# Where the flags of far sampling points are made in a fused deformable-convolution, attention and expert block

## The chip, the cores and the metric

The kernel runs on one core of one Trainium2 chip. The metric is the device time of one execution in microseconds (us). TensorE is called PE below (PEld is its weight load), VectorE is DVE, ScalarE is ACT, GpSimd is POOL and SyncE is SP.

## The reference, cut to what matters

Input x has shape (4, 32, 32, 128): 4 images of 32 x 32 positions with 128 channels. The first layer is a deformable convolution (3 x 3, so 9 points, for each of 8 groups of 16 channels):

```
x1 = silu(bn(depthwise_conv(gn(x))))
offset = x1 @ off_w + off_b                       # (N, H, W, 8, 9, 2)
mask = softmax((x1 @ mask_w + mask_b).reshape(N, H, W, G, P), -1)
samples = _bilinear_sample(img, sg)               # img = gn(x) @ in_w + in_b, padded
out = (samples * m).sum(-1)
return out @ out_w + out_b
```

It is followed by an attention layer over the 1024 positions of each image and by a layer of experts. The change touches the first layer alone.

## The kernel before, in words

The deformable convolution is worked off in 8 chunks of 4 image rows (ROWS = 4, CHUNKS = 8). An offset up to 2 in size (REACH) is handled without a gather: each point's bilinear weight is written as "hats" over 5 taps in x and in y, the mask multiplies the y hats, their outer products are added into a 7 x 7 stencil for each position and group, and the output is the sum over the 49 stencil positions of stencil times shifted input. Points with an offset above 2 in size ("far" points) are few. They are flagged, listed and then repaired by POOL with indirect DMAs.

For a chunk the engines work so:

- DVE ends the silu (finish_silu), so that PE can make 3 x 72 raw offsets and mask logits for each of 4 rows in PSUM (offsets, pair 0).
- ACT (prepare) copies them to SBUF (off), squares the offsets (far_xy, in the tile outer), makes the first 2 of 5 taps of the hats, waits for DVE's shifted logits, takes their exp, makes 3 more taps and finishes all hats with a Relu.
- DVE (mask_logits, masks, weigh_hats) takes the logits' maximum over 9 points, subtracts it in 4 instructions, takes the larger of the two squares, compares it with 4 and so has flags (far); it then sums the exps, divides, and multiplies the y hats.
- DVE (stencils) makes 9 outer products and 8 additions. Between all these instructions stand the products of the chunk before (products), in 28 units of two stencil positions (every fourth unit is one position). A call fill(n) issues n units; STENCIL_FILL says how many follow each addition. A row of seven positions is used in rotation (PROD = 7), so DVE can be seven positions ahead of PE.
- PE (add_up) adds each position's product up by 4 transposing matmuls. At set positions in the 49 it does other work in between, in program order: at AT_FAR it counts the flags of the next chunk over the partitions (count_far), at AT_CONV and the 8 positions behind it one of the 9 depthwise matmuls each (convolve), at AT_SAMPLES the repair (add_fix), at AT_PROJECT the output projection of the chunk before (project, 12 matmuls). At the head of each turn stand the offset matmuls of the next chunk (offsets).
- DVE lists the largest counts (list_far), ACT stores them (count_out), POOL reads the list.

There are 7 turns, each with the products of chunk k and the preparation of chunk k + 1; the last chunk's products stand alone behind them. In a turn DVE's order is: finish_silu, fill(5), mask_logits, fill(1), masks, weigh_hats, stencils, the rest of the units, and the first two units of the next chunk. Units are called u0 to u27 below; u6 is the fifth unit of fill(5), u24 holds positions 42 and 43, the last ones ahead of AT_PROJECT = 44.

Of the kernel before, what the change touches and what calls it, by code (L numbers as in the profile page):

```python
# [61 lines left out]
AT_FAR, AT_CONV, AT_SAMPLES, AT_PROJECT = 18, 22, 36, 44  # L62
# [5 lines left out]
STENCIL_FILL = (0, 1, 1, 0, 1, 1, 0, 1, 1)  # L68
# [17 lines left out]
FAR_UNIT = 8192.0  # L86

# [41 lines left out]
def hybrid_block_kernel(nc, x, in_w, in_b, out_w, out_b, off_w, off_b, mask_w, mask_b, dw_k, bn_g, bn_b,  # L129
                        bn_m, bn_v, attn_w, wr, br, w1, b1, w2, b2, gamma, beta, out):  # L130
    padded = nc.dram_tensor("padded", (WP, B, HP, C), F32, kind="Internal").ap()
    with ExitStack() as ctx:
# [3 lines left out]
        def sem(name):  # L136
# [24 lines left out]
        bias_parts = sb("bias_parts", [1, 3, 3 * GP + C], BF16)  # L161
# [23 lines left out]
        off_most = sb("off_most", [P, ROWS * GP])  # L185

        far = sb("far", [P, FAR_COLS], BF16)
        far_flags = far[:, :]
# [5 lines left out]
        far_xy = outer[:, :, :, :].rearrange("p g a b -> p (g a b)")[:, 0:ROWS * 2 * GP] \  # L194
            .rearrange("p (r o) -> p r o", r=ROWS)
# [120 lines left out]
        square_done = sem("square_done")  # L316
# [14 lines left out]
        masks_done = sem("masks_done")  # L331
# [163 lines left out]
        def _(sc):  # L495
# [34 lines left out]
            def prepare(k):  # L530

                sc.wait_ge(off_mm, k + 2)
                if not isinstance(k, int) or k > 0:
                    sc.wait_ge(fix_done, k)
                sc.sem_inc(act_waited, 1)
                raw = pair[0][:, :].rearrange("p (r o) -> p r o", r=ROWS)
                sc.activation(off[:, bass.ds(k % OFFS, 1), :, :].rearrange("p s r o -> p (s r) o"),
                              raw[:, :, 0:3 * GP], ACT.Copy).then_inc(off_done, 1)

                sc.wait_ge(hats_used, k + 1)  # L540
                sc.activation(far_xy, raw[:, :, 0:2 * GP], ACT.Square).then_inc(square_done, 1)
                sc.wait_ge(off_done, k + 1)
                sc.sem_inc(act_waited, 1)
                for t in range(TAPS):
                    if t == EXP_AT:
                        sc.wait_ge(logits_done, k + 1)
                        sc.sem_inc(act_waited, 1)
                        mf = mask[:, :, :].rearrange("p g q -> p (g q)")
                        sc.activation(mf, mf, ACT.Exp).then_inc(exp_done, 1)
                    own(sc.activation(  # L550
                        hats[:, :, :, t].rearrange("p a (r g) -> p a r g", r=ROWS),
                        off[:, bass.ds(k % OFFS, 1), :, 0:2 * GP].rearrange("p s r (a g) -> p a (s r) g", a=2),
                        ACT.Abs, bias=tap_bias[:, t:t + 1]))
                own.wait()
                hf = hats[:, :, :, :].rearrange("p a g t -> p (a g t)")
                sc.activation(hf, hf, ACT.Relu, bias=tap_bias[:, TAPS:TAPS + 1], scale=-1.0).then_inc(hats_done, 1)

# [133 lines left out]
        def _(pe):  # L691
# [23 lines left out]
            def offsets(k):  # L715
# [3 lines left out]
                if not isinstance(k, int) or k > 0:  # L719
                    pe.wait_ge(square_done, k)  # L720
# [37 lines left out]
            def count_far(k):  # L758

                pe.wait_ge(masks_done, k + 1)  # L760
                if not isinstance(k, int) or k > 0:
                    pe.wait_ge(far_done, k)
                    pe.wait_ge(listed, k)
                count = pair[1][:, 0:FAR_COLS]
                pe.matmul(count, ones16[:, :], far[:, :], start=True, stop=False)
                pe.matmul(count, ones[0:1, :], far_codes[:, :], start=False, stop=True).then_inc(far_mm, 1)
# [209 lines left out]
        def _(gp):  # L976
# [11 lines left out]
            own(gp.memset(ones16[:, :], 1.0))  # L988
            own(gp.memset(group_mean[:, :], 1.0 / GN_C))
# [24 lines left out]
            for r in range(ROWS):  # L1014
                gp.iota(far_codes[:, r * GP:(r + 1) * GP].rearrange("p (g q) -> p g q", g=G),
                        pattern=[[GROUP_UNIT + PTS, G], [1, PTS]], base=r * G * GROUP_UNIT, **whole)
# [102 lines left out]
            with gp.Fori(0, CHUNKS) as k:  # L1119
# [9 lines left out]
                more = gp.value_load(far_list_i[0:1, LIST - 1:LIST], min_val=0, max_val=int(FAR_UNIT) * (P + 1) - 1)  # L1129
                with gp.If(more > int(FAR_UNIT) - 1):  # L1130
                    with gp.Fori(0, ROWS * G) as rg:
                        with gp.Fori(0, PTS) as q:
                            count = gp.value_load(far_counts[0:1, bass.ds(k % 2, 1), bass.ds(rg * PTS + q, 1)]
                                                  .rearrange("a s o -> a (s o)"), min_val=0,
                                                  max_val=int(FAR_UNIT) * (P + 1) - 1)
# [4 lines left out]
                with gp.Else():  # L1140
                    with gp.Fori(0, LIST - 1) as j:
                        code = gp.value_load(far_list_i[0:1, bass.ds(j, 1)], min_val=0, max_val=int(FAR_UNIT) * (P + 1) - 1)
# [43 lines left out]
        def _(ve):  # L1186
# [64 lines left out]
            def mask_logits(k, fill):  # L1251
# [5 lines left out]
                for r in range(ROWS):  # L1257
                    last = ve.tensor_tensor(mask[:, r * G:(r + 1) * G, :], lg[:, r],
                                            row_max[:, r * G:(r + 1) * G].unsqueeze(2).to_broadcast([P, G, PTS]),
                                            ALU.subtract)  # L1260
                last.then_inc(logits_done, 1)

                ve.wait_ge(square_done, k + 1)
                own(ve.tensor_tensor(off_most[:, :].rearrange("p (r g) -> p r g", r=ROWS), far_xy[:, :, 0:GP],
                                     far_xy[:, :, GP:], ALU.max))
                fill(1)
                own.wait()
                own(ve.tensor_scalar(far_flags, off_most[:, :], float(REACH) ** 2, FAR_UNIT, ALU.is_gt, ALU.mult))
                fill(1)
                own.wait()  # L1270
# [3 lines left out]
            def masks(k, fill):  # L1274
# [5 lines left out]
                ve.sem_inc(masks_done, 1)  # L1280
# [89 lines left out]
            def turn(k, first):  # L1370
# [8 lines left out]
                fill(5)  # L1379
# [235 lines left out]
```

## Time and profile before

| | |
|---|---|
| time, median of 3 runs | 721.9 us (720.75 to 722.38) |
| profiled execution, its own time | 724.42 us |
| its span | 722.7 us |
| PE busy | 593.9 us, 82% |
| DVE busy | 580.6 us, 80% |
| ACT busy | 227.1 us, 31% |
| POOL busy | 306.8 us, 42% |
| mean granted clock of PE | 0.908 of full |

Busy time is the time in which an engine worked; a matmul's end is modelled, so a busy PE isn't PE at its peak. The seven turns and the last chunk's products lie between about 66 and 460 us of the span; before them stand the input normalisation and the first chunk's preparation, behind them the attention and the experts.

### The profile page before, as it was taken

Reading aid. Unit: us, or ns where it says so; the run is one execution under the profiler, and the core shown is the slowest. Engines: PE = TensorE matmul, PEld = TensorE weight load, DVE = VectorE, ACT = ScalarE, POOL = GpSimd, SP = SyncE. Lnnn points to the kernel's source line nnn. Section 1 sums busy time; section 2 is a strip of 40 time slices with the busy share of each in tenths; the row PEclk is TensorE's granted clock in tenths of the full one; section 3 lists DMA queues with packets and bytes.
Section 4 is the critical chain, followed back from the end, with each engine's and each line's share of the span. In section 5 each row is a group of like instructions: output and inputs, shape, how many; then the busy total and the mean of one; then the engine's idle time right before and its main releaser. Section 6 shows DMA issues by size and latency. Waiting matters only on the chain.

```text
span 722.7 us, 11093 instructions
## 1 busy us (share of the span) xinstructions
PE 593.9 (82%) x3456; PEld 444.2 (61%) x3456; DVE 580.6 (80%) x1052; ACT 227.1 (31%) x332; POOL 306.8 (42%) x326
## 2 busy tenths in 40 slices
PE   4982878869859869869959589779999999939995
PEld 3452656557547558557547477647777777725674
DVE  4489899998997997998999999456777766752766
ACT  6150502413314314215206000144445444413431
POOL 7523795897348793058068240021221221125111
PEclk9796988998998987988999779989999999977998
DMA  6057503003003006000000000000000000004111
GB/s 182 29 212 269 169 1 103 3 1 103 1 1 103 2 2 254 1 1 2 1 1 3 0 1 1 1 0 1 1 1 1 1 0 1 1 3 115 30 45 44
DMA packets 25595, 30.54 MB, mean 42 GB/s; under 512 B 5189, under 2 KB 17685, under 8 KB 25557
## 3 DMA queue, kind: packets, MB, share of 16 engines
q1 hardware_dynamic: 24654, 29.77, 12.5%
q0 software_dynamic: 896, 0.23, 0.4%
q8 instruction: 27, 0.44, 0.3%
q14 instruction: 12, 0.09, 0.0%
q10 hardware_dynamic: 6, 0.00, 0.0%
HBM read 24.94 MB, written 5.05 MB: 42 GB/s over the span
## 4 chain that ended last, share of the span: by engine, by line
PE 55%; DVE 20%; issue 10%; DVEq 2%; ACT 1%; POOL 0%; POOLq 0%; ACTq 0%
PE banks L777 14%; DVE prod L1355 9%; PE banks L887 8%; PE pair L867 8%; PE pair L932 4%; PE pair L730 4%; PE banks L877 4%; PE banks L966 3%; DVE stencil L1331 3%; DVE outer L1325 3%; PE banks L795 3%; PE pair L723 2%; PE banks L793 2%; PE banks L859 1%; DVE hats L1292 1%
## 5 line engine op out<-in xcount | busy, mean ns | idle before, releaser
L777 PE MATMUL banks<-ident,prod 128*128 128x128 f32 x1568 | 225.2, 295 | 81.5 <-DVE prod L1355 80.8
L777 PEld LDWEIGHTS banks<-ident,prod 128*128 128x128 f32 x1568 | 192.7, 152 | 136.1 <-DVE prod L1355 112.5
L1355 DVE TENSOR_TENSOR prod<-shifted,stencil 128x1024 f32 (+1 forms) x224 | 238.8, 1089 | 17.3 <-PE banks L777 14.5
L1123 POOL CAST far_list_i<-far_list 1x8 int32<-1x8 f32 x8 | 40.5, 5066 | 105.5 <-DVE far_list L1341 86.1
L1151 POOL TENSOR_TENSOR rstd_now<-mv_now,neg_half 128x2 f32<-128x2 f32 x32 | 22.9, 717 | 135.6 <-DVE mv_now L1407 135.6
L730 PE MATMUL pair<-xg,dw_diag 128*128 128x512 f32 x144 | 73.4, 611 | 1.7 <-ACT dw_diag L511 1.7
L887 PEld LDWEIGHTS banks<-shifted 128*128 128x128 f32 x512 | 60.2, 192 | 8.1 <-issue 6.1
L887 PE MATMUL banks<-shifted 128*128 128x128 f32 x512 | 63.3, 277 | 2.3 <-ACT shifted L639 1.4
L1325 DVE TENSOR_TENSOR outer<-hats 128x800 f32<-128x800 f32 x64 | 63.2, 987 | 0.8
L1331 DVE TENSOR_TENSOR stencil<-stencil,outer 128x800 f32 (+1 forms) x64 | 62.9, 983 | 0.3
L867 PE MATMUL pair<-shifted 128*128 128x512 f32 x128 | 60.4, 596 | 0.6 <-ACT shifted L622 0.6
L1422 DVE TENSOR_REDUCE neg_max<-pair 128x1 f32<-128x1024 f32 x32 | 39.2, 1224 | 23.6 <-PE pair L867 22.5
L550 ACT ACTIVATE hats<-off,tap_bias 128x576 f32 (+1 forms) x40 | 48.3, 1335 | 0.0
L634 ACT ACTIVATE shifted<-pair,neg_max 128x1024 f32<-128x1024 f32 x32 | 35.6, 1114 | 36.6 <-DVE neg_max L1422 36.6
L1088 POOL DMA_INDIRECT got<-padded,cell_now x28 | 40.7, 1455 | 8.4 <-issue 6.4
L1427 DVE COPY shifted<-banks 128x512 f32<-128x512 f32 x32 | 22.1, 689 | 15.6 <-PE banks L877 15.6
L569 ACT ACTIVATE res<-banks 128x512 f32 (+1 forms) x8 | 4.8, 599 | 91.0 <-PE banks L795 91.0
L877 PE MATMUL banks<-ident,shifted 128*128 128x128 f32 x256 | 33.2, 273 | 0.0
L523 ACT ACTIVATE gate<-pair,bn_fold 128x512 f32<-128x512 f32 x8 | 6.2, 778 | 84.1 <-issue 66.3
L867 PEld LDWEIGHTS pair<-shifted 128*128 128x128 f32 x128 | 21.9, 190 | 16.8 <-issue 15.8
L932 PE MATMUL pair<-shifted,stage 128*128 128x512 f32 x64 | 31.4, 640 | 0.0
L1157 POOL TENSOR_TENSOR res<-res,bias_all 128x256 f32 x16 | 11.6, 727 | 46.2 <-DVE xg L1413 46.2
(229 smaller groups left out, 871.6 us busy)
## 6 DMA issues: line engine op xcount, KB each, us to landing
shifted<-padded SPq DMA_DIRECT2D x42, 256.0 KB
shifted<-padded SPq DMA_DIRECT2D x14, 640.0 KB
res<-in_x_dram SPq DMA_DIRECT2D x4, 512.0 KB, 5.7
padded<-stage SPq DMA_DIRECT2D x4, 512.0 KB, 2.7
stage<-in_L_ffn_W_dram SPq DMA_DIRECT2D x16, 128.0 KB, 2.1
out_dram<-res SPq DMA_DIRECT2D x8, 256.0 KB, 2.3
padded<-stencil SPq DMA_DIRECT2D x2, 228.0 KB, 2.5
got<-padded,cell_now POOLq DMA_INDIRECT x28
```

The costliest lines, as they stand in the source:

```text
L550: own(sc.activation(hats[:, :, :, t].rearrange("p a (r g) -> p a r g", r=ROWS), off[:, bass.ds(k % OFFS, 1), :, 0:2 * GP].rearrange("p s r ...
L730: mm = pe.matmul(conv_bank.rearrange("c (r a) -> c r a", r=ROWS), dw_diag[:, t, :], src, start=(t == 0), stop=(t == 8))
L777: mm = pe.matmul(acc_of(c, r), prod[:, d % PROD, r * G:(r + 1) * G, :].rearrange("p g c -> p (g c)"), ident[:, :], is_transpose=True, star ...
L867: mm = pe.matmul(pair[s][:, h * 512:(h + 1) * 512], keyed[:, bass.ds(i * P, P)], normed_t[:, bass.ds((i // TILES) * TOK + h * 512, 512)], ...
L877: mm = pe.transpose(bank[h][:, m * P:(m + 1) * P], probs[:, s, (4 * h + m) * P:(4 * h + m + 1) * P], ident[:, :])
L887: mm = pe.matmul(bank[2][:, 0:C], probs_t[:, m * P:(m + 1) * P], normed[:, bass.ds((i // TILES) * TILES + m, 1), :].rearrange("p t c -> p ...
L932: pe.matmul(pair[f // 2][:, (f % 2) * 512:(f % 2 + 1) * 512], w1_sel[:, 2 * n + f // 2, (f % 2) * P:(f % 2 + 1) * P], normed2_t[:, q * 512 ...
L1088: gp.indirect_dma_start(out=got[:, a, :], out_offset=None, in_=table, in_offset=bass.IndirectOffsetOnAxis(ap=cell_now[:, a:a + 1], axis=0) ...
L1123: gp.tensor_copy(far_list_i[:, :], far_list[:, :]).then_inc(point, 1)
L1325: own(ve.tensor_tensor(to if q == 0 else outer[:, :, :, :], hy[:, :, q, :].unsqueeze(3).to_broadcast(full), hx[:, :, q, :].unsqueeze(2).to ...
L1331: own(ve.tensor_tensor(to, to, outer[:, :, :, :], ALU.add))
L1355: ins = ve.tensor_tensor(prod[:, dx:dx + n, :, :], shifted[:, dx:dx + n, bass.ds(((c % HALF) * ROWS + dy) * G, ROWS * G), :], stencil_of[: ...
```

## The change

The flags are made another way. ACT no longer squares the offsets. Behind the Relu of the hats it makes two tiles of signs from the raw offsets in PSUM, sign(x - 2) and sign(-x - 2), in bfloat16. PE adds up the four sign pieces (two signs, x and y) over the partitions with a column of 8192, into one partition, with a base of 4 x 128 x 8192 in the codes: the result is 8192 or more just where a point is far. DVE's maximum and comparison are gone, and the subtraction of the logits' maximum is one instruction in place of four. The two units of products that stood between the removed instructions now stand ahead of the logits' maximum (fill(7) for fill(5)), one of the last units of the stencil has moved ahead with them (STENCIL_FILL ends in 0), and the count on PE stands three positions later (AT_FAR 21 for 18) and waits for the signs. ACT's write of the signs waits for PE's count of the chunk before. The small tile bias_parts lies in the signs' storage.

```diff
-AT_FAR, AT_CONV, AT_SAMPLES, AT_PROJECT = 18, 22, 36, 44
+AT_FAR, AT_CONV, AT_SAMPLES, AT_PROJECT = 21, 22, 36, 44
-STENCIL_FILL = (0, 1, 1, 0, 1, 1, 0, 1, 1)
+STENCIL_FILL = (0, 1, 1, 0, 1, 1, 0, 1, 0)
...
# ACT, prepare
-                sc.activation(far_xy, raw[:, :, 0:2 * GP], ACT.Square).then_inc(square_done, 1)
...
                 sc.activation(hf, hf, ACT.Relu, bias=tap_bias[:, TAPS:TAPS + 1], scale=-1.0).then_inc(hats_done, 1)
+                if not isinstance(k, int) or k > 0:
+                    sc.wait_ge(far_mm, k)
+                    sc.sem_inc(act_waited, 1)
+                for i, sign in enumerate((1.0, -1.0)):
+                    last = sc.activation(signs[:, i, :, :], raw[:, :, 0:2 * GP], ACT.Sign,
+                                         bias=tap_bias[:, TAPS - 1:TAPS], scale=sign)
+                last.then_inc(signs_done, 1)
...
# PE, offsets
-                    pe.wait_ge(square_done, k)
+                    pe.wait_ge(signs_done, k)
# PE, count_far
-                pe.wait_ge(masks_done, k + 1)
+                pe.wait_ge(signs_done, k + 1)
...
-                count = pair[1][:, 0:FAR_COLS]
-                pe.matmul(count, ones16[:, :], far[:, :], start=True, stop=False)
-                pe.matmul(count, ones[0:1, :], far_codes[:, :], start=False, stop=True).then_inc(far_mm, 1)
+                count = pair[1][0:1, 0:FAR_COLS]
+                pe.matmul(count, ones[0:1, 0:1], far_codes[:, :], start=True, stop=False)
+                for i in range(4):
+                    mm = pe.matmul(count, far_unit[:, :], signs[:, i // 2, :, (i % 2) * GP:(i % 2 + 1) * GP],
+                                   start=False, stop=(i == 3))
+                mm.then_inc(far_mm, 1)
...
# DVE, mask_logits
-                for r in range(ROWS):
-                    last = ve.tensor_tensor(mask[:, r * G:(r + 1) * G, :], lg[:, r],
-                                            row_max[:, r * G:(r + 1) * G].unsqueeze(2).to_broadcast([P, G, PTS]),
-                                            ALU.subtract)
-                last.then_inc(logits_done, 1)
-                ve.wait_ge(square_done, k + 1)
-                own(ve.tensor_tensor(off_most[:, :].rearrange("p (r g) -> p r g", r=ROWS), far_xy[:, :, 0:GP],
-                                     far_xy[:, :, GP:], ALU.max))
+                ve.tensor_tensor(mask[:, :, :].rearrange("p (r g) q -> p r g q", r=ROWS), lg,
+                                 row_max[:, :].rearrange("p (r g) -> p r g", r=ROWS).unsqueeze(3)
+                                 .to_broadcast([P, ROWS, G, PTS]), ALU.subtract).then_inc(logits_done, 1)
                 fill(1)
-                own.wait()
-                own(ve.tensor_scalar(far_flags, off_most[:, :], float(REACH) ** 2, FAR_UNIT, ALU.is_gt, ALU.mult))
-                fill(1)
-                own.wait()
...
# DVE, masks
-                ve.sem_inc(masks_done, 1)
...
# DVE, turn
                 finish_silu(k + 1)
-                fill(5)
+                fill(7)
                 mask_logits(k + 1, fill)
```

The program's order on DVE in the first turn, from the maximum of the logits (row_max) to the last unit ahead of the weighing of the hats; prod is a unit of products, 128x512 a unit of one position. Before:

```order
L1254 TENSOR_REDUCE row_max<-off 128x32
L1355 TENSOR_TENSOR prod<-shifted,stencil 128x512
L1258 TENSOR_TENSOR mask<-off,row_max 128x72 x4
L1264 TENSOR_TENSOR off_most<-outer 128x288
L1355 TENSOR_TENSOR prod<-shifted,stencil 128x1024
L1268 TENSOR_SCALAR far<-off_most 128x288
L1355 TENSOR_TENSOR prod<-shifted,stencil 128x1024 x2
L1277 TENSOR_REDUCE row_sum<-mask 128x32
L1355 TENSOR_TENSOR prod<-shifted,stencil 128x512
L1281 RECIPROCAL row_sum<-row_sum 128x32
L1282 TENSOR_TENSOR off<-mask,row_sum 128x4x72
L1355 TENSOR_TENSOR prod<-shifted,stencil 128x1024
```

The same place in the changed program, begun two units earlier:

```order
L1356 TENSOR_TENSOR prod<-shifted,stencil 128x512
L1356 TENSOR_TENSOR prod<-shifted,stencil 128x1024
L1264 TENSOR_REDUCE row_max<-off 128x32
L1356 TENSOR_TENSOR prod<-shifted,stencil 128x1024
L1267 TENSOR_TENSOR mask<-off,row_max 128x288
L1356 TENSOR_TENSOR prod<-shifted,stencil 128x1024
L1356 TENSOR_TENSOR prod<-shifted,stencil 128x512
L1279 TENSOR_REDUCE row_sum<-mask 128x32
L1356 TENSOR_TENSOR prod<-shifted,stencil 128x1024
L1282 RECIPROCAL row_sum<-row_sum 128x32
L1283 TENSOR_TENSOR off<-mask,row_sum 128x4x72
L1356 TENSOR_TENSOR prod<-shifted,stencil 128x1024
```

Two units have moved from behind the subtraction to ahead of the row's maximum, and a further one stands ahead of the weighing; between the subtraction and the weighing there are now four units in place of five.

On PE the same turn, from the adding up behind the offset matmuls to the second of the nine depthwise matmuls (dw_diag); four matmuls onto banks are one stencil position. Before:

```order
L777 MATMUL banks<-ident,prod 128x128 x56
L765 MATMUL pair<-far,ones 128x288
L766 MATMUL pair<-far_codes,ones 128x288
L777 MATMUL banks<-ident,prod 128x128 x16
L730 MATMUL pair<-xg,dw_diag 128x512
L777 MATMUL banks<-ident,prod 128x128 x4
L730 MATMUL pair<-xg,dw_diag 128x512
```

And in the changed program:

```order
L786 MATMUL banks<-ident,prod 128x128 x68
L771 MATMUL pair<-far_codes,ones 1x288
L773 MATMUL pair<-signs,far_unit 1x288 x4
L786 MATMUL banks<-ident,prod 128x128 x4
L736 MATMUL pair<-xg,dw_diag 128x512
L786 MATMUL banks<-ident,prod 128x128 x4
L736 MATMUL pair<-xg,dw_diag 128x512
```

The count has moved three positions later, to just one position ahead of the depthwise matmuls, and has five matmuls in place of two.

## Rows read from the trace of the kernel before

**Rows 1.** Waits of DVE over the span: us in total, times, longest.

```profile
DVE prod L1355 <- PE banks L777: 14.5, 12, 2.1
...
DVE prod L1355 <- issue: 2.6, 1, 2.6
```

**Rows 2.** Timeline of DVE: start, us, instruction, [idle before it <- releaser].

```profile
74.61 1.22 DVE L1355 TENSOR_TENSOR prod<-shifted,stencil 128x1024 f32<-128x1024 f32 x1 [1.74 <-PE banks L777]
...
124.50 1.23 DVE L1355 TENSOR_TENSOR prod<-shifted,stencil 128x1024 f32 x1 [0.57 <-PE banks L777]
...
223.26 1.23 DVE L1355 TENSOR_TENSOR prod<-shifted,stencil 128x1024 f32 x1 [2.62 <-issue]
...
230.65 1.23 DVE L1355 TENSOR_TENSOR prod<-shifted,stencil 128x1024 f32 x1 [1.55 <-PE banks L777]
...
431.98 27.01 DVE L1355 TENSOR_TENSOR prod<-shifted,stencil 128x1024 f32 x27 [0.20 <-PE banks L777]
```

**Rows 3.** Timeline of DVE, end of one turn and head of the next.

```profile
213.84 0.98 DVE L1331 TENSOR_TENSOR stencil<-stencil,outer 128x800 f32 x1
...
214.74 1.21 DVE L1355 TENSOR_TENSOR prod<-shifted,stencil 128x1024 f32 x1
...
215.87 1.00 DVE L1325 TENSOR_TENSOR outer<-hats 128x800 f32<-128x800 f32 x1
...
216.80 1.21 DVE L1355 TENSOR_TENSOR prod<-shifted,stencil 128x1024 f32 x1
...
232.76 0.66 DVE L1258 TENSOR_TENSOR mask<-off,row_max 128x72 f32<-128x72 f32 x4
233.33 0.45 DVE L1264 TENSOR_TENSOR off_most<-outer 128x288 f32<-128x288 f32 x1
...
233.70 1.32 DVE L1355 TENSOR_TENSOR prod<-shifted,stencil 128x1024 f32 x1
...
234.94 0.36 DVE L1268 TENSOR_SCALAR far<-off_most 128x288 bf16<-128x288 f32 x1
...
235.22 2.37 DVE L1355 TENSOR_TENSOR prod<-shifted,stencil 128x1024 f32 x2
...
240.36 1.65 DVE L1292 TENSOR_TENSOR hats<-hats,off 128x1440 f32<-128x1440 f32 x1
```

**Rows 4.** Groups by line and shape, DVE: busy us, mean ns | idle before.

```profile
L1282 DVE TENSOR_TENSOR off<-mask,row_sum 128x288 f32 x6 | 2.8, 471 | 0.2
```

**Rows 5.** Timeline of ACT in the same turn.

```profile
230.54 0.65 ACT L541 ACTIVATE outer<-pair 128x576 f32<-128x576 f32 x1
231.07 2.50 ACT L550 ACTIVATE hats<-off,tap_bias 128x576 f32 x2
233.53 0.45 ACT L549 ACTIVATE mask<-mask 128x288 f32<-128x288 f32 x1
...
237.47 2.70 ACT L556 ACTIVATE hats<-hats,tap_bias 128x2880 f32<-128x2880 f32 x1
```

**Rows 6.** Timeline of PE, four turns' pieces.

```profile
213.97 1.97 PE L777 MATMUL banks<-ident,prod 128*128 128x128 f32 x8 [2.63 <-DVE prod L1355]
...
291.95 0.75 PE L766 MATMUL pair<-far_codes,ones 1*128 1x288 f32 x2
...
299.52 0.60 PE L777 MATMUL banks<-ident,prod 128*128 128x128 f32 x4
...
300.82 0.60 PE L777 MATMUL banks<-ident,prod 128*128 128x128 f32 x4
...
401.64 4.24 PE L777 MATMUL banks<-ident,prod 128*128 128x128 f32 x20 [2.99 <-DVE prod L1355]
```

**Rows 7.** Windows of PE: length, busy (instructions), granted clock, DMA share, GB/s.

```profile
402.50:405.00 2.50, 2.39 (x13) 0.54 0.00 0
405.00:407.50 2.50, 1.12 (x9) 1.00 0.00 0
213.00:221.00 8.00, 7.03 (x28) 0.54 0.06 11
```

More of the change, by code:

```diff
@@ L86 @@
 FAR_UNIT = 8192.0
+MOST_CODE = int(FAR_UNIT) * (4 * P + 1) - 1
 PAIRS = B * H // ROWS // 2
@@ L159, in hybrid_block_kernel @@
         bias_all = sb("bias_all", [P, 3, C])
-        bias_parts = sb("bias_parts", [1, 3, 3 * GP + C], BF16)
         bias_parts3 = sb("bias_parts3", [3, 3 * GP + C], BF16)
@@ L184, in hybrid_block_kernel @@
         off_of = off[:, :, :, :].rearrange("p s r o -> p s (r o)")
-        off_most = sb("off_most", [P, ROWS * GP])
-        far = sb("far", [P, FAR_COLS], BF16)
-        far_flags = far[:, :]
+        signs = sb("signs", [P, 2, ROWS, 2 * GP], BF16)
+        bias_parts = signs[0:1, :, :, :].rearrange("p s r o -> p (s r o)")[:, 0:3 * (3 * GP + C)] \
+            .rearrange("p (i o) -> p i o", i=3)
+        far_unit = sb("far_unit", [P, 1], BF16)
         row_max = sb("row_max", [P, ROWS * G])
@@ L193, in hybrid_block_kernel @@
         outer = sb("outer", [P, ROWS * G, TAPS, TAPS])
-        far_xy = outer[:, :, :, :].rearrange("p g a b -> p (g a b)")[:, 0:ROWS * 2 * GP] \
-            .rearrange("p (r o) -> p r o", r=ROWS)
         stencil = sb("stencil", [P, 2, ROWS * G * STENCIL])
@@ L315, in hybrid_block_kernel @@
         bias_in = sem("bias_in")
-        square_done = sem("square_done")
+        signs_done = sem("signs_done")
         stencil_clear = sem("stencil_clear")
@@ L330, in hybrid_block_kernel @@
         hats_done = sem("hats_done")
-        masks_done = sem("masks_done")
         far_mm = sem("far_mm")
@@ L988, in _ @@
             own(gp.memset(ones16[:, :], 1.0))
+            own(gp.memset(far_unit[:, :], FAR_UNIT))
             own(gp.memset(group_mean[:, :], 1.0 / GN_C))
@@ L1015, in _ @@
                 gp.iota(far_codes[:, r * GP:(r + 1) * GP].rearrange("p (g q) -> p g q", g=G),
-                        pattern=[[GROUP_UNIT + PTS, G], [1, PTS]], base=r * G * GROUP_UNIT, **whole)
+                        pattern=[[GROUP_UNIT + PTS, G], [1, PTS]], base=int(FAR_UNIT) * 4 * P + r * G * GROUP_UNIT, **whole)
             gp.iota(corner[:, :].rearrange("p (a b) -> p a b", a=2), pattern=[[B * HP * G, 2], [G, 2]], base=0, **whole)
@@ L1128, in _ @@
                 gp.sem_inc(list_taken, 1)
-                more = gp.value_load(far_list_i[0:1, LIST - 1:LIST], min_val=0, max_val=int(FAR_UNIT) * (P + 1) - 1)
+                more = gp.value_load(far_list_i[0:1, LIST - 1:LIST], min_val=0, max_val=MOST_CODE)
                 with gp.If(more > int(FAR_UNIT) - 1):
@@ L1134, in _ @@
                                                   .rearrange("a s o -> a (s o)"), min_val=0,
-                                                  max_val=int(FAR_UNIT) * (P + 1) - 1)
+                                                  max_val=MOST_CODE)
                             with gp.If(count > int(FAR_UNIT) - 1):
@@ L1141, in _ @@
                     with gp.Fori(0, LIST - 1) as j:
-                        code = gp.value_load(far_list_i[0:1, bass.ds(j, 1)], min_val=0, max_val=int(FAR_UNIT) * (P + 1) - 1)
+                        code = gp.value_load(far_list_i[0:1, bass.ds(j, 1)], min_val=0, max_val=MOST_CODE)
                         with gp.If(code > int(FAR_UNIT) - 1):
```

## The prediction

> **What bounds the kernel now.** I read the page first: DVE and PE are each busy for four fifths of the span, so neither can be ruled out. Then the waits of DVE. In the part that the change touches DVE waits almost only for room for its products: 14.5 us in 12 waits for PE, and 2.6 us in one that the profile puts down to no one [rows 1]; together 17.1 us. The timeline shows where they lie [rows 2]. One of 1.74 us stands in the first turn at 74.6 us. The others stand where a turn ends and the next begins: at its smallest end 0.57 us, at its largest 2.62 + 1.55 = 4.17 us, and 0.20 us ahead of the last chunk's products. With the first taken off, 15.4 us are left for seven turn ends, 10.4 of them at the four ends that I have not named. Each such wait follows the same piece of PE: u24 arrives late (PE has been idle for 2.63 us ahead of it, at 213.97), PE adds its two positions, does the projection, adds, does the next offsets, and then frees the slots for u1 and u6 [rows 6]. From 213.97 to 230.65 this chain is PE's: 16.7 us. All the rest of a turn, from u6 to the next u24, is DVE's. There PE, ACT and POOL are ahead. So a turn is a stretch of DVE plus a stretch of PE, and each edit is to be priced by the stretch in which it lies.
>
> **DVE's removed work.** Starts of instructions on DVE give what one costs in a row of others. The four subtractions take 232.76 to 233.33, 0.57 us; the maximum 233.33 to 233.70, 0.37; the comparison 234.94 to 235.22, 0.28 [rows 3]. The new subtraction has 288 elements a partition with a broadcast operand, as the weighting of the mask has, which takes 471 ns [rows 4]; the maximum of 450 ns occupied 0.37 us, so I give the new one 0.38. (Bounds: 0.35 to 0.57, the four together.) A turn loses 0.57 - 0.38 + 0.37 + 0.28 = 0.84 us of DVE's stretch, seven turns 5.9 us. The first chunk's preparation, ahead of the turns, waits for ACT's hats in any case; I give it nothing.
>
> **The hats come later.** ACT's exp starts 0.77 us behind the first subtraction's start (232.76, 233.53) [rows 3, 5]. From there to the end of the Relu it is 237.47 + 2.70 - 233.53 = 6.64 us of ACT, all of it needed before DVE can weigh the hats. Before, DVE arrived there at 240.36 and the hats were ready at 240.17: a balance with 0.2 us to spare. Let S be the start of the new subtraction. It ends at S + 0.47, the exp begins 0.1 later, the hats are ready at S + 7.2. DVE's way from the first instruction behind the subtraction to the weighing was 240.36 - 233.33 = 7.03 us. It loses the maximum (0.37), the comparison (0.28) and one unit of products (four units there for five; 214.74 to 215.87 is 1.13 [rows 3]), so it is 5.25, and DVE arrives at S + 5.6. It then waits 1.6 us, in every turn: 7 x 1.6 = 11.2 us. That ACT has no square any more (0.53 us, 230.54 to 231.07 [rows 5]) doesn't help, since the exp waits for the logits, which the two units ahead of the row's maximum delay further.
>
> **The moved units.** The one unit that left the end of the stencil brings u24 ahead: it now follows the outer product of the seventh point and no longer that of the eighth. An addition (213.84 to 214.74, 0.90) and an outer product (215.87 to 216.80, 0.93) thus lie behind u24 [rows 3], that is, beside PE's chain instead of ahead of it. That takes 1.8 us out of a turn as long as DVE has such a wait to fill: 0.57 at the smallest end, 0.20 at the last, 1.8 at the largest, and, as the 10.4 us at four ends are 2.6 each on average and not even, 1.7 at each of these. Sum 0.57 + 0.2 + 1.8 + 6.8 = 9.4 us gained.
>
> **The count on PE.** The signs read the 576 elements that the square read, so they cost ACT 0.53 each in a row and 0.65 for the last [rows 5]. They start behind the Relu (3.94 us after the exp, plus its 2.6), at S + 7.1, and end at S + 8.3. PE comes to the count when position 20 is added. That unit is the second behind the subtraction, done at about S + 2.1, added at S + 2.6. PE then stands still for 5.7 us. What is queued behind the count on PE: everything, so all slots. Seven positions can be made ahead, 21 to 27, which lasts DVE beyond S + 13, so the wait itself costs nothing. The count then takes between 0.75 (the old codes alone [rows 6]) and about 2; I take 1.5. Its successors are nine positions, each with a depthwise matmul, one per 1.30 us (299.52 to 300.82 [rows 6]) against one per about 1.0 of DVE. Laid out from S, unit 18 (positions 32, 33) needs position 26 added and finds it with some 0.7 us to spare: u18 starts at S + 17.7, position 26 is added at S + 17.0.
>
> That holds at full clock. The trace has a PE wait of 2.99 us ahead of 401.64, and in the window from 402.5 the granted clock is 0.54, that is mostly the lower level of 1.2 GHz, and 1.00 from 405 [rows 6, 7]: half clock for some 3.2 us after PE took up work. A wait of 5.7 us I expect to do the same or more. Half clock for 3.2 us is 1.6 us of PE's work; less the 0.7 to spare, 0.9 us of DVE in each of the six turns with depthwise matmuls: 5.4 us. The bounds are 0 (the clock holds or comes back within 1.4 us) and, with half clock for 7 us, 2.8 a turn, 16.8 in all.
>
> **The projection's clock.** In the window 213 to 221 the granted clock is 0.54 [rows 7], so the projection ran at half clock, behind PE's 2.63 us of idleness. With u24 one outer product behind u23 that idleness is gone. Of the 15.4 us, 9.4 are already filled; of the remaining 6 a full clock would remove all but a few tenths a turn, about 4. I take 3.0, between 0 and 4.
>
> **A rule against the change.** An ACT sign of 576 elements takes 0.65 us where DVE's maximum and comparison of 288 pairs take 0.45 and 0.36 [rows 3, 5]. The Trainium skill, ScalarE: Activation LUTs, section "Rules for kernel authors", says to give relu, max, min, add and mul to VectorE rather than ScalarE, which is slower per element. If ACT were what a turn waits for as a whole, two signs for one square would add 0.53 us a chunk, 4 us in all, in place of the 5.9 gained. ACT is idle between chunks for far longer than that, so the sum has nothing for it.
>
> **Sum.** -5.9 (work) + 11.2 (hats) - 9.4 (moved units) + 5.4 (clock behind the count) - 3.0 (projection) = -1.7 us. The profiled execution took 724.42 us, its span 722.7; that becomes 722.7 and 721.0. The median of the runs is 2.5 us below the profiled one: 721.9 - 1.7 = **720.2 us**.
>
> **Rivals.**
> - *The wait at the count is free* (chance 0.22). PE's clock holds or returns at once, so the 5.4 us fall away: 714.8. For it: PE's work after the wait is dense, matmuls of 512 columns. Against it: waits half as long stand ahead of half clock in the trace.
> - *The count's half clock becomes the bound* (0.33), the case on the other side. PE resumes at half clock for 5 to 7 us, in front of the nine depthwise matmuls which have only 0.7 us of room. At 5 us it costs 2.5 - 0.7 = 1.8 a turn, 10.8 in all, and with the projection's clock unimproved: -5.9 + 11.2 - 9.4 + 10.8 = +6.7, so 728.6; at 7 us 734. It decides (no gain left) from about 4 us of half clock on.
> - *The hats' wait doesn't come* (0.05), if ACT's exp and hats run into less than 6.64 us or DVE's units there are slower. Then 11.2 us fall away: 709.
> - *The change doesn't do what it says for the projection* (inside the forecast's range): the idleness ahead of u24 goes, and the clock is half all the same. Then 3.0 us are missing: 723.2.
>
> **How the numbers follow.** The forecast has the remaining chance, 0.40, and a range of its own of 717.5 to 723.5 (the projection's 0 to 4, and a third of the count's 5.4 either way). A measurement of this kernel can tell about 0.2%, 1.4 us, from no change: 720.5 and 723.3 are the borders. The forecast's case gives 0.20 faster, 0.15 same, 0.05 slower; the free wait and the missing wait of the hats 0.27 faster; the half clock 0.02 same and 0.31 slower. Faster 0.47, same 0.17, slower 0.36. The range of 8 in 10 reaches from the free wait to the middle of the half-clock case: 713.5 to 729.
>
> **What would show it.** In the changed kernel's profile: no rows for the maximum and comparison, one subtraction of about 0.47 us; DVE waiting about 1.6 us for ACT's Relu ahead of the weighing of the hats in each turn; PE idle for about 5.7 us, ended by ACT's signs, and half clock behind it; DVE waits for PE at u17 or u18 of about a microsecond; waits at u1 and u6 that have shrunk from 15.4 to 3 us or less; no wait of PE of over 2 us ahead of the projection, and a granted clock above 0.9 there. It would be wrong if the wait of the hats were absent, or if PE's clock behind the count stayed at 1.00 or at half for over 4 us.

## The result: 2.1% slower

The changed kernel takes 737.25 us (735.0 to 739.6, 4 runs) against 722.14 us (720.75 to 724.77, 4 runs): a ratio of 1.0214, with a 95% interval of 1.0186 to 1.0242. Forecast were 720.2 us and a range that ended at 729. The profiled execution took 735.0 us, its span is 733.2 us, 10.5 more than before. Of this the seven turns and the last chunk's products have 12.9: from the first turn's u6 (before 74.61, now 73.02) to the end of the last product (before 431.98 + 27.01 = 458.99, now 470.25). What lies ahead of them and behind is 2.4 us shorter.

The waits of DVE and of PE over the span of the changed kernel, which answer to [rows 1] (engine, line, whom it waited for: us in total, times, longest):

```profile
DVE prod L1356 <- PE banks L786: 20.1, 26, 2.3
DVE hats L1293 <- ACT hats L553: 13.2, 8, 1.7
...
DVE prod L1356 <- DVE stencil L1332: 2.0, 5, 0.4
...
PE pair L771 <- ACT signs L560: 37.3, 7, 5.3
```

Two waits are new in the turns: DVE's for the hats, and PE's of 5.3 us at the count, where it stood for 0.5 us in the kernel before (its row stands below). A third, of 0.4 us, is DVE's for its own last addition (row L1332).

```profile
PE pair L765 <- DVEq L1280: 3.3, 7, 0.5
```

DVE's waits for room in the products were 17.1 us in 13 pieces and are 22.1 with those that the profile puts down to DVE's own last addition, in 31 pieces.

One turn on DVE, which answers to [rows 3]:

```profile
182.59 1.21 DVE L1356 TENSOR_TENSOR prod<-shifted,stencil 128x1024 f32 x1
183.73 0.45 DVE L1267 TENSOR_TENSOR mask<-off,row_max 128x288 f32<-128x288 f32 x1
184.10 1.81 DVE L1356 TENSOR_TENSOR prod<-shifted,stencil 128x1024 f32 x2
...
188.08 1.22 DVE L1356 TENSOR_TENSOR prod<-shifted,stencil 128x1024 f32 x1
191.01 1.66 DVE L1293 TENSOR_TENSOR hats<-hats,off 128x1440 f32<-128x1440 f32 x1 [1.72 <-ACT hats L553]
...
198.26 1.22 DVE L1356 TENSOR_TENSOR prod<-shifted,stencil 128x1024 f32 x1 [0.85 <-PE banks L786]
201.33 1.23 DVE L1356 TENSOR_TENSOR prod<-shifted,stencil 128x1024 f32 x1 [0.95 <-PE banks L786]
203.93 1.22 DVE L1356 TENSOR_TENSOR prod<-shifted,stencil 128x1024 f32 x1 [0.47 <-PE banks L786]
...
225.87 2.51 DVE L1356 TENSOR_TENSOR prod<-shifted,stencil 128x1024 f32 x2 [0.43 <-DVE stencil L1332]
235.43 2.98 DVE L1356 TENSOR_TENSOR prod<-shifted,stencil 128x1024 f32 x3 [2.28 <-PE banks L786]
```

The reader sees the subtraction at 183.73 and occupying 0.37 us (the next unit starts at 184.10), the wait of 1.72 us for the hats, three waits for room at u16, u17 and u18, and at the turn's end 0.43 and 2.28 us. The same turn on ACT and PE, which answers to [rows 5, 6]:

```profile
184.29 0.44 ACT L546 ACTIVATE mask<-mask 128x288 f32<-128x288 f32 x1 [2.54 <-DVE mask L1267]
184.64 3.54 ACT L547 ACTIVATE hats<-off,tap_bias 128x576 f32 x3
188.21 2.69 ACT L553 ACTIVATE hats<-hats,tap_bias 128x2880 f32<-128x2880 f32 x1
190.81 1.35 ACT L560 ACTIVATE signs<-pair,tap_bias 128x576 bf16<-128x576 f32 x2
```
```profile
192.22 1.11 PE L771 MATMUL pair<-far_codes,ones 1*1 1x288 f32 x2 [5.33 <-ACT signs L560]
193.26 1.12 PE L773 MATMUL pair<-signs,far_unit 128*1 128x288 bf16 x4
194.31 1.12 PE L786 MATMUL banks<-ident,prod 128*128 128x128 f32 x4
195.22 1.92 PE L736 MATMUL pair<-xg,dw_diag 128*128 128x512 f32 x2
...
199.69 1.02 PE L736 MATMUL pair<-xg,dw_diag 128*128 128x512 f32 x2
...
217.74 1.97 PE L786 MATMUL banks<-ident,prod 128*128 128x128 f32 x8 [1.22 <-DVE prod L1356]
```

ACT stood for 2.54 us until the logits came, and its hats and signs follow without a gap. PE stood for 5.33 us, and the first depthwise matmul behind it took 1.92 us where a later one takes 1.02. The windows of PE in that turn (length, busy, granted clock as a share of 2.4 GHz, DMA share, GB/s), which answer to [rows 7]:

```profile
187.50:190.00 2.50, 0.00 (x0) 1.00 0.00 0
190.00:192.50 2.50, 0.28 (x1) 0.93 0.00 0
192.50:195.00 2.50, 2.50 (x9) 0.50 0.00 0
195.00:197.50 2.50, 2.50 (x8) 0.50 0.00 0
197.50:200.00 2.50, 2.50 (x10) 0.70 0.00 0
...
220.00:222.50 2.50, 2.50 (x11) 0.50 0.00 0
```

The clock fell to 1.2 GHz at the end of PE's wait, came back only within 197.5 to 200 (0.70 there is full clock for the last two fifths, from 199.0), some 6.8 us behind PE's restart at 192.22, and was at the lower level again in the projection (220). By such windows the same happened in each of the six turns with depthwise matmuls; the half clock behind PE's restart lasted 3.9 to 6.8 us, 5.4 on average, so the turn shown is the longest.

### The profile page after: what moved, and what is told of

The parts are those of the page before. It is cut to its first block and busy times, and to the rows that moved or that the text cites. A ratio compares the mean times of both kernels' runs of the same rounds, so it can differ in the third digit from the quotient of the medians.

```text
span 733.2 us, 11078 instructions
## 1 busy us (share of the span) xinstructions
PE 598.9 (82%) x3480; PEld 444.3 (61%) x3480; DVE 576.2 (79%) x1012; ACT 233.9 (32%) x340; POOL 281.8 (38%) x327
## 5 line engine op out<-in xcount | busy, mean ns | idle before, releaser
L786 PE MATMUL banks<-ident,prod 128*128 128x128 f32 x1568 | 221.8, 295 | 52.5 <-DVE prod L1356 51.9
L1356 DVE TENSOR_TENSOR prod<-shifted,stencil 128x1024 f32 (+1 forms) x224 | 238.7, 1091 | 22.1 <-PE banks L786 20.1
L1133 POOL CAST far_list_i<-far_list 1x8 int32<-1x8 f32 x8 | 36.9, 4610 | 145.6 <-DVE far_list L1342 126.3
L736 PE MATMUL pair<-xg,dw_diag 128*128 128x512 f32 x144 | 78.6, 648 | 1.2 <-ACT dw_diag L509 1.2
L1332 DVE TENSOR_TENSOR stencil<-stencil,outer 128x800 f32 (+1 forms) x64 | 63.0, 984 | 0.3
L771 PE MATMUL pair<-far_codes,ones 1*1 1x288 f32 x16 | 8.4, 625 | 37.3 <-ACT signs L560 37.3
L736 PEld LDWEIGHTS pair<-xg,dw_diag 128*128 128x128 f32 x144 | 25.6, 212 | 11.1 <-issue 11.1
```

What stands on the lines that cost most here:

```text
L736: mm = pe.matmul(conv_bank.rearrange("c (r a) -> c r a", r=ROWS), dw_diag[:, t, :], src, start=(t == 0), stop=(t == 8))
L786: mm = pe.matmul(acc_of(c, r), prod[:, d % PROD, r * G:(r + 1) * G, :].rearrange("p g c -> p (g c)"), ident[:, :], is_transpose=True, star ...
L1133: gp.tensor_copy(far_list_i[:, :], far_list[:, :]).then_inc(point, 1)
L1332: own(ve.tensor_tensor(to, to, outer[:, :, :, :], ALU.add))
L1356: ins = ve.tensor_tensor(prod[:, dx:dx + n, :, :], shifted[:, dx:dx + n, bass.ds(((c % HALF) * ROWS + dy) * G, ROWS * G), :], stencil_of[: ...
```

## The experiments

**The logits early again.** The two units that the change put ahead of the row's maximum stand behind the subtraction.

```diff
-                fill(7)
+                fill(5)
...
                                  .to_broadcast([P, ROWS, G, PTS]), ALU.subtract).then_inc(logits_done, 1)
-                fill(1)
+                fill(3)
```

> The changed kernel with fill(5) ahead of the logits' maximum and fill(3) behind the subtraction: the two units stand behind the logits again, everything else as changed. Theory A (the lost time is the wait for the hats, 1.7 us a turn, plus the half clock behind the count): the wait for the Relu falls from 13.2 us to under 2, PE's wait at the count shrinks from 5.3 to about 3.5 us, time 722 to 726 us. Theory B (the wait for the hats only took the place of waits at the turns' ends, which come back when it is gone): 733 us or more, with waits for room of 20 us and more.

Measured: 717.46 us (10 runs), ratio to the kernel before 0.9954 (0.9935 to 0.9974), 19.8 us below the changed kernel's 737.25. Its waits:

```profile
DVE prod L1356 <- PE banks L786: 13.5, 16, 2.3
...
DVE hats L1293 <- ACT hats L553: 1.2, 1, 1.2
...
PE pair L771 <- ACT signs L560: 21.2, 7, 3.1
```

This is less than the 722 to 726 us expected. The wait for the hats is left in the first chunk alone, PE's wait at the count is 3.0 us on average, and DVE's waits for room fell too. The spans differ by 18.2 us: 12.0 for the hats in the turns, and 5.8 for room (22.1 to 16.3, with DVE's own last addition). With the shorter wait of PE the first depthwise matmul took 1.02 us, full clock, in three of six turns; in the changed kernel it did in none. Theory B is out. The place of two units decides the sign of the whole change: ahead of the logits they make it 2.1% slower than the kernel before, behind them 0.5% faster.

**The count late.** PE counts behind the nine depthwise matmuls.

```diff
-AT_FAR, AT_CONV, AT_SAMPLES, AT_PROJECT = 21, 22, 36, 44
+AT_FAR, AT_CONV, AT_SAMPLES, AT_PROJECT = 31, 22, 36, 44
...
-                add_up(k, first_of(BEGIN), AT_FAR)
-                for i in range(AT_FAR, STENCIL):
+                add_up(k, first_of(BEGIN), AT_CONV)
+                for i in range(AT_CONV, STENCIL):
```

> The changed kernel with the count behind the nine depthwise matmuls (AT_FAR 31). Theory A: PE has no wait of 5.3 us any more, its clock stays at 1.00 through the depthwise matmuls, DVE's waits of 0.5 to 0.9 us at u16 to u18 (9.4 us in all) vanish, the wait for the hats stays at 1.7 a turn: 726 to 729 us. Theory B (the half clock is a symptom, the turn is limited by the sum of PE's work): waits for room of DVE stay near 20 us and the time at 734 or more.

Measured: 724.15 us (10 runs), ratio 1.0052 (1.0022 to 1.0082), 13.1 below the changed kernel and somewhat below the 726 to 729 expected. DVE's waits:

```profile
DVE prod L1356 <- PE banks L786: 14.2, 8, 2.9
DVE hats L1293 <- ACT hats L553: 13.4, 8, 1.8
```

None of the 8 waits for room is at u16 to u18 any more, and PE has no wait for the signs. The hats' wait is as it was. The 9.4 us of waits at u16 to u18 are gone, but those at the turns' ends grew by some 4, so that all waits for room fell by 5.5 us (22.1 to 16.6); the spans differ by 7.7 us, the medians by more.

**The signs first.** They stand where the square stood, ahead of the hats, with the count at 21.

```diff
+                if not isinstance(k, int) or k > 0:
+                    sc.wait_ge(far_mm, k)
+                    sc.sem_inc(act_waited, 1)
+                for i, sign in enumerate((1.0, -1.0)):
+                    last = sc.activation(signs[:, i, :, :], raw[:, :, 0:2 * GP], ACT.Sign,
+                                         bias=tap_bias[:, TAPS - 1:TAPS], scale=sign)
+                last.then_inc(signs_done, 1)
                 sc.wait_ge(hats_used, k + 1)
...
# the same seven lines are gone behind the Relu
```

> The changed kernel with the two signs made where the square was, ahead of the hats, while ACT waits for the logits anyway. Theory A: the signs are ready before PE comes to the count, so no PE wait and no half clock there; the wait for the hats is unchanged since the exp still waits for the logits: 726 to 729 us, like the late count. If the signs delay the hats instead, the wait for the Relu grows from 1.7 to about 2.8 a turn and the gain is gone.

Measured: 728.55 us (10 runs), ratio 1.0087 (1.0055 to 1.0118). In the turns it is the late count over again: the waits of DVE are 14.3 us for room and 13.4 for the hats. The medians differ from the late count's by 4.4 us, the spans by 3.2, and these lie ahead of the turns: the first u6 starts at 75.68 against 72.44, with PE's mean clock in the first 75 us at 0.80 against 0.86. That is hardly the signs' doing: the kernel with both repairs (below), whose signs stand behind the hats, has 0.80 and 75.17 there as well, which leaves them 0.5 us. Why the clock ahead of the turns differs between these kernels is not known.

**Seven and thirteen useless matmuls ahead of the wait.** PE waits until the same moment but works in between.

```diff
+                if not isinstance(k, int) or k > 0:
+                    pe.wait_ge(far_done, k)
+                    pe.wait_ge(listed, k)
+                    for i in range(7):        # 13 in the second kernel
+                        pe.matmul(pair[1][:, 0:3 * GP], ident[:, :], offmask_w[:, :], start=True, stop=True)
                 pe.wait_ge(signs_done, k + 1)
```

> The changed kernel with seven useless matmuls of 216 columns on PE ahead of its wait at the count, in the count's own bank, which the count overwrites: PE still waits for the signs until the same moment, but works in between. Theory A (it is the half clock and not the wait that delays DVE): granted clock 1.00 in the depthwise matmuls, DVE's waits at u16 to u18 fall from 9.4 us to under 3, 729 to 732 us. Theory C (the late start of nine depthwise matmuls alone does it): waits at u16 to u18 stay, 736 us or more.

> The changed kernel with thirteen useless matmuls of 216 columns ahead of the wait at the count, some 5 us at full clock, in place of the seven that filled only 2.7 us and left 2.8 us of idleness and half clock behind it. Theory A: the clock stays at 1.00 through the depthwise matmuls, DVE's waits at u16 to u18 fall under 1 us in all; if these waits set the time, it is 728 to 731 us. Theory D (they only move to the turn's end): the waits go but the time stays at 735 to 738.

Measured with seven: 736.97 us (4 runs), ratio 1.0202 (1.0157 to 1.0246), nothing gained where 5 us or more were expected. They filled 2.7 us; PE then still stood and its clock still fell. The useless matmuls, the count and the first depthwise matmul on PE's timeline:

```profile
189.53 2.72 PE L770 MATMUL pair<-offmask_w,ident 128*128 128x216 f32 x14
195.04 0.64 PE L776 MATMUL pair<-far_codes,ones 1*1 1x288 f32 x2 [2.79 <-ACT signs L560]
...
196.74 1.92 PE L736 MATMUL pair<-xg,dw_diag 128*128 128x512 f32 x2
```

The lower level lasted less long, so the waits at u17 and u18 fell to 0.34 and 0.47 us in most turns and those at u16 to u18 from 9.4 to 6.1 us in all (3.3 went, and not the 6 that an expectation below says), but at u6 five of the six turn ends now have 1.8 to 2.3 us, where in the changed kernel three have: all waits for room are 22.3 us, as in the changed kernel (22.1).

Measured with thirteen: 727.97 us (7 runs), ratio 1.0061 (1.0026 to 1.0096), 9.3 us below the changed kernel, and 8.4 below the changed kernel on the same chip (next). The waits of DVE and PE, then the same place on the timeline, then a window:

```profile
DVE prod L1361 <- PE banks L791: 12.4, 9, 2.9
...
PE pair L776 <- ACT signs L560: 3.6, 6, 0.6
```
```profile
188.11 4.91 PE L770 MATMUL pair<-offmask_w,ident 128*128 128x216 f32 x26
193.63 0.64 PE L776 MATMUL pair<-far_codes,ones 1*1 1x288 f32 x2 [0.60 <-ACT signs L560]
...
195.27 1.02 PE L736 MATMUL pair<-xg,dw_diag 128*128 128x512 f32 x2
```
```profile
197.50:200.00 2.50, 2.50 (x13) 1.00 0.00 0
```

PE's wait ends at the same place, at the signs, and 91 more matmuls are in the program; yet the kernel is 8 to 9 us faster, and the waits at u16 to u18 are gone. So it was PE's clock behind the wait and not the wait itself.

**The changed kernel once more**, beside the second of these.

> The changed kernel itself, on the same chip as the runs beside it: 735 to 739 us.

Measured: 736.35 us (4 runs), ratio 1.019 (1.0136 to 1.0244). Its waits for room are 22.5 us in all; with the thirteen matmuls they are 14.8. This second trace of the changed kernel also shows how far two executions differ: at u16 to u18 it has 12.2 us, where the first has 9.4, and at the turns' ends 7.9, where the first has 10.4.

**Both repairs**: the logits early (fill(5), fill(3)) and the count at 31, as in the first two diffs.

> The changed kernel with both repairs: the two units behind the logits (fill(5), fill(3)) and the count behind the depthwise matmuls (AT_FAR 31). Theory A (waits add up): the waits of 0.3 to 0.7 us at u16 to u18 that the early logits alone left, 4 us in all, go as well: 713 to 715 us. Theory D (what is taken from the waits at the count comes back as waits at the turn's end, as seven useless matmuls showed, where 6 us of the one went and 4 us of the other came): 716 to 719 us.

Measured: 714.04 us (4 runs), ratio 0.9881 (0.9842 to 0.9921). That is 3.4 us less than the early logits alone, as expected if the waits add up. The two traces show less of it: the 4.0 us of waits at u16 to u18 are gone, but the turns' ends have 1.8 us more, and the spans differ by 1.0 us only (the profiled execution of both repairs, 715.74 us, was the slowest of its four).

**The moved unit put back**, on both repairs.

```diff
-STENCIL_FILL = (0, 1, 1, 0, 1, 1, 0, 1, 0)
+STENCIL_FILL = (0, 1, 1, 0, 1, 1, 0, 1, 1)
...
-                fill(3)
+                fill(2)
```

> Both repairs, and the moved unit put back at the end of the stencil (STENCIL_FILL as before, fill(2) behind the subtraction), so that u24 follows one addition and one outer product later. Prediction's theory: 1.8 us a turn come back onto DVE's stretch where a wait covered them, 5 to 9 us more than with both repairs alone. Rival: the unit's place gives less than half of that, because DVE then waits 0.33 us more at the end of a turn for its own last addition, and PE's chain is longer: 0 to 3 us more.

Measured: 723.9 us (10 runs), ratio 1.0016 (0.9988 to 1.0044), 9.9 us more than both repairs. Its waits, with those of both repairs behind them:

```profile
DVE prod L1356 <- PE banks L786: 20.2, 12, 2.7
...
DVE hats L1293 <- ACT hats L553: 5.2, 8, 1.2
```
```profile
DVE prod L1356 <- PE banks L786: 12.2, 10, 2.3
...
DVE prod L1356 <- DVE stencil L1332: 2.0, 5, 0.4
...
DVE hats L1293 <- ACT hats L553: 1.0, 1, 1.0
```

Two causes share the 9.9 us: 4.2 more of waiting for the hats, since one unit fewer stands between the logits and the weighing, and 20.2 - 14.2 = 6.0 more of waiting at the turns' ends. Expected were 5 to 9 us in all, so the sum came out above it; the part that is the moved unit's own, by waits at the turns' ends, is 6 us.

**One subtraction alone**, on the kernel before (the diff is that of the change in mask_logits, without the rest).

> The kernel before with one change, the subtraction in one instruction. Prediction's term: 0.19 us in each of seven turns, 1.3 us less, 719 to 721. Rival: nothing, since the exp waits for the two hats on ACT anyway and a wait for the Relu takes the place.

Measured: 724.57 us (10 runs), ratio 1.0026 (0.9999 to 1.0054). No gain: 1.3 us less was expected (0.19 in each of seven turns), and the interval excludes it. The waits for the hats are as before (0.3 us), so they did not take the place; the waits for room are 19.1 us in this trace against 17.1.

**Useless matmuls ahead of the projection**, on both repairs.

```diff
                     add_up(k, i, i + 1)
+                    if not first and 33 <= i < AT_PROJECT - 1:
+                        pe.wait_ge(res1_done, k)
+                        for w in range(2):
+                            pe.matmul(bank[0][:, 0:P], ident[:, :], ident[:, :], start=True, stop=True)
```

> Both repairs, and two useless matmuls of 128 columns on PE behind each of positions 33 to 42, where PE otherwise waits for products, into the bank that the projection overwrites. Theory E (the half clock in the projection and the adding behind it, entered through PE's idleness ahead of it, makes the waits of about 2 us at u6): granted clock 1.00 through the projection, waits at u6 of 0.6 us or less, 3 to 8 us less than with both repairs alone. Rival: the useless matmuls delay the products' adding and cost as much as they give, same time or more.

Measured: 714.43 us (4 runs), ratio 0.9891 (0.9852 to 0.9929), the same as both repairs. Windows of PE and rows of PE and DVE at two turns' ends show why:

```profile
162.50:172.50 10.00, 7.93 (x52) 1.00 0.59 188
...
207.50:210.00 2.50, 2.06 (x16) 1.00 0.00 0
...
217.50:220.00 2.50, 2.50 (x13) 0.50 0.91 303
```
```profile
173.58 1.23 DVE L1360 TENSOR_TENSOR prod<-shifted,stencil 128x1024 f32 x1 [0.57 <-PE banks L786]
...
217.36 3.50 PE L786 MATMUL banks<-ident,prod 128*128 128x128 f32 x16 [1.90 <-DVE prod L1360]
...
224.91 1.22 DVE L1360 TENSOR_TENSOR prod<-shifted,stencil 128x1024 f32 x1 [1.86 <-PE banks L786]
```

The projection ran at full clock; PE then was through early and stood for 1.90 us until the next chunk's first products. At four of the five turn ends with a projection its clock fell there instead, ahead of the offset matmuls, and the waits at u6 are 1.86 to 1.98 us. At the fifth the clock held from the projection through the offset matmuls (162.5 to 172.5), with the same stand of PE, and the wait at u6 is 0.57 us (173.58). The changed kernel's own turn ends agree: 0.58 us where the mean clock from the projection's end to the offsets' end is 0.90 or 1.00, 1.76 to 2.28 where it is 0.73 or 0.74 (and 0.94 to 0.98 at 0.89 in its second trace). So full clock in the projection alone is worth nothing; where it also holds behind the projection, up to the offsets, the wait at u6 is 1.2 us shorter or more.

**The new order alone**, on the kernel before: flags by DVE as ever.

```diff
-STENCIL_FILL = (0, 1, 1, 0, 1, 1, 0, 1, 1)
+STENCIL_FILL = (0, 1, 1, 0, 1, 1, 0, 1, 0)
...
                 own(ve.tensor_scalar(far_flags, off_most[:, :], float(REACH) ** 2, FAR_UNIT, ALU.is_gt, ALU.mult))
-                fill(1)
...
-                fill(5)
+                fill(7)
```

> The kernel before with the new order of the units alone (fill(7), none of the two units between maximum, comparison and what follows replaced, STENCIL_FILL ending in 0); flags made by DVE as before, four subtractions, count at 18. Theory A: the logits come two units later, so DVE waits some 0.9 us a turn for the hats (the maximum and comparison fill the rest), 6.5 us; the unit moved ahead of the projection gives back 6 us as it did with both repairs: 720 to 724. If the order is harmless without the signs: 716 or less, from the moved unit.

Measured: 726.76 us (10 runs), ratio 1.0069 (1.0039 to 1.0099), slower and above what was expected. The hats' wait is there without any signs, 0.6 to 0.7 us in six of the turns, and so is a wait of PE at the count, 2.6 us against 0.5 before:

```profile
DVE prod L1354 <- PE banks L777: 15.6, 10, 2.9
DVE hats L1291 <- ACT hats L556: 6.1, 8, 1.0
```
```profile
PE pair L765 <- DVEq L1279: 18.0, 7, 2.6
```

Half clock stands behind that wait of PE too: the first of the two rows of the first depthwise matmul took 0.70 to 1.06 us in all six turns, where the kernel before has 0.59. The moved unit gave nothing back here: the waits for room are 17.6 us with DVE's own last addition, as before (17.1), and not 6 us less.

**The last addition covered**, on both repairs: u24 stays where the change put it, and u27 stands behind the last addition again.

```diff
-STENCIL_FILL = (0, 1, 1, 0, 1, 1, 0, 1, 0)
+STENCIL_FILL = (0, 1, 1, 0, 1, 1, 0, 0, 1)
```

> Both repairs, and u27 back behind the last addition while u24 stays where the change put it (STENCIL_FILL ends in 0, 0, 1): the 0.43 us that DVE waits for its own last addition at each turn's end is covered. Theory: 0.33 us in seven turns, 2.3 us less than with both repairs, 711 to 713. Rival: the turns' ends are PE's there, so the wait for room grows by as much and the time stays at 714.

Measured: 708.18 us (706.1 to 714.98, 4 runs), ratio 0.9836 (0.977 to 0.9901), the fastest of all, and 5.9 us below both repairs where 2.3 were expected. (One of its four runs took 714.98 us, so the intervals of the two ratios overlap; the other three are 4.6 us or more below the fastest run of both repairs.) Its waits for room:

```profile
DVE prod L1356 <- PE banks L786: 6.0, 7, 2.3
```

After the first (2.29 us) one is left per turn, 0.57 us at u6 in five of the six. PE's clock in the turns is 0.96 on average, against 0.90 with both repairs, and at five turn ends it is 1.00 from the projection through the offsets; these are the five with 0.57 us. PE's stand behind the projection is 1.0 to 1.2 us there, against 1.9 in the kernel with useless matmuls ahead of the projection; whether this is why the clock holds was not tried.

## Why the prediction was wrong

Its terms, against the waits of the two profiles (us, the seven turns and the last chunk's products):

| term | forecast | measured |
|---|---|---|
| removed work of DVE | -5.9 | about -3.5 (what the others leave of 12.9) |
| wait for the hats | +11.2 | +12.0 |
| waits at u16 to u18, half clock behind the count | +5.4 | +9.4 |
| waits at the turns' ends: moved unit | -9.4 | -5.0, with the next |
| the projection's clock | -3.0 | |
| sum | -1.7 | +12.9 |

From forecast to measured the turns' ends have 7.4 us of the error (12.4 were to go, 5.0 went), the clock behind the count 4.0, the removed work 2.4 and the hats 0.8.

**Right.** The wait for the hats: 1.6 us a turn were forecast from two rows of ACT and two of DVE, 1.63 to 1.74 came, and the early logits took it away. The order alone on the old kernel has 0.6 to 0.7 us of it without any signs, so that part belongs to the order. Of the other 1.0 us, 0.65 are the maximum and the comparison, which no longer stand between the subtraction and the weighing: work taken from there comes back as a wait. PE's wait at the count: 5.7 forecast, 5.3 measured. The signs took ACT 1.35 us for two, where 0.53 + 0.65 = 1.18 were read from the square.

**The step that failed first** is the clock behind the count. The mechanism was right, and the thirteen useless matmuls show it: take PE's idleness away and leave the wait, and 8 to 9 us come back. The size was wrong. I took 3.2 us of half clock from the one place in the trace with an idleness of 2.99 us [rows 6, 7] as typical for one of 5.7; it was 5.4 us on average and 6.8 in the turn shown, and the waits were 1.56 us a turn on average of six and 2.27 in that turn, not 0.9. The rows at hand had a longer one: behind 2.63 us of idleness the window from 213 to 221 has a granted clock of 0.54 [rows 6, 7], which is some 7 us of half clock, and the prediction used it for the projection alone. By the prediction's own formula 5.4 us would cost 5.4 / 2 - 0.7 = 2.0 us a turn, so the formula is on the high side. This is the rival of the half clock, which had a chance of 0.33; it gave 728.6 for 5 us of half clock and 734 for 7.

**The second step** is the turns' ends, where 12.4 us were to go and 5.0 went. The projection's clock, -3.0, did not come: PE still stood for 1.22 us ahead of u24 in the turn shown, and ran the projection at 0.50 at four of the five turn ends that have one. And the term was in the wrong place: the useless matmuls ahead of the projection show that full clock in it removes nothing where the clock falls behind it, and that the wait at u6 goes down to 0.57 us where it holds up to the offsets. The moved unit was oversized. Put back, it cost 6.0 us of waits. I let the ends fall to a few tenths, but they have floors in the changed kernel: 0.57 us at u6, behind the offset matmuls, and 0.43 ahead of u0, where DVE waits for its own last addition since the change took the unit behind it away. The prediction didn't see this second wait at all, though the order of the program shows it; covering it gave 5.9 us, part of which is the better clock of PE at the turns' ends.

**The removed work** came out 2.4 us short, if what the other terms leave is put down to it; the subtraction alone, on the kernel before, gave nothing. The subtraction does occupy 0.37 us where four took 0.57, and the maximum and comparison are gone. The rest is likely the overlap that a wait takes away: in a row of instructions DVE starts the next 0.08 us ahead of the end of the last (213.84 + 0.98 against 214.74 [rows 3]), behind a wait it doesn't, and the changed kernel has some 25 waits more, 2 us. This is argued, not tried.

The spans differ by 10.5 us, the medians by 15.1. The profiled execution was the fastest of the changed kernel's four (735.0, the others 736.58 to 739.6), and that of before, 724.42 us, was 2.3 above its median of 722.14. So the table explains the 10.5 us between two single executions; the other 4.6 us of the medians' difference lie in how far these two are from their medians.

## What to carry to other kernels

When instructions are removed between a producer's signal and the consumer of its answer, the filler that stood between them has to stay there: two units moved ahead of the signal cost 12 us of waiting and, through the longer wait of PE for the same answer, some 6 more in the traces (8 by the medians). Price a wait of PE in front of dense matmuls with the clock that it will have afterwards, and where an idle PE can't be avoided, place the wait behind the dense part and not ahead of it. And look for the wait of an engine for its own last instruction wherever a filler is taken from the end of a chain.

## What the hardware showed that was not expected

- Useless work made the kernel faster: thirteen matmuls of 216 columns a turn in PE's idleness (4.91 us of work) lower the time from 736.35 to 727.97 us. Seven, which leave 2.79 us of idleness, gain nothing (736.97).
- Idleness of 5.3 us of PE had 3.9 to 6.8 us of half clock behind PE's restart in the six turns of the changed kernel, 5.4 on average. In the changed kernel PE's clock was 0.86 on average between 75 and 445 us of the span, before 0.90, and in the fastest kernel 0.96.
- An idleness of 2.85 to 3.12 us in the same place (the early logits) left the clock up for the depthwise matmuls in three of six turns, while 2.8 us behind seven useless matmuls did in none of the six. What else decides it stays open.
